# Expert results scattered to rows in token order, and read back with plain transfers in place of gathers

## The chip, the cores and the metric

The kernel runs on one core of one Trainium2 chip. The metric is the device time of one execution in microseconds (us). Five engines work side by side: TensorE (PE, with its weight loads shown as PEld), VectorE (DVE), ScalarE (ACT), GpSimd (POOL) and SyncE (SP, which only issues transfers). Transfers run on 16 DMA engines; SP's go through one queue (q1 in the profile, "hardware_dynamic"), POOL's through another (q0, "software_dynamic").

## The reference

The input is 8 sequences of 1024 rows of 256 floats (8192 tokens). Four layers follow, each with a residual sum and a layer norm:

```
x = ln(x + linear_attention(x))     # 32 heads
x = ln(x + moe0(x))                 # 8 experts, the last a no-op; top 2; capacity 1024 rows per expert
x = ln(x + attention(x))            # softmax attention, one head of 256
x = ln(x + moe1(x))                 # 8 small experts and a shared one
```

In `moe0` each of the seven real experts takes the first 1024 tokens that chose it, computes `relu(x @ w_in) @ w_out` for them, and the result, times the token's gate, is added to the token. A token's first or second choice that found no room, or that was the no-op expert, adds nothing from that expert's product. So a token has two result rows to add, of which either may be absent.

## The kernel before

All floating products are split into a high and a low part of the operands and take three fp32r matmuls each (`product`, L114 to L121; `accumulate`, L124).

**Stage A** (`stage_a`, L182 to L822, some 0 to 433 us of the span) does the first layer and the routing of the second, one sequence of 1024 rows per step, eight steps and two shorter ones for what lags behind. The order of units within a step is written out by hand (`ORDER`, L194), and every engine follows it in its own program. POOL begins with constants (L392 to L434), then subtracts to make `xT_lo` (`split_xT`, L437), adds the bias to the loaded rows (`bias`, L442) and marks slots (`mark`, L449). The router gives each chosen pair a slot number: expert times 1024 plus position, or a row of zeros past the end (`TRASH`) where there is no room. The slots are stored to memory, 8 KB a step (L359). An inverse table `inv` (128 x 56), slot to token, is built with matmuls: POOL marks in which lane and column each of the 16 x 128 pairs of the step lies (`mark_slots`, L332), ACT multiplies the column marks by the row number (L528, one instruction) and by the tile number (L530, eight instructions of 128 x 112, since the tile number is the same for a token's first and second choice), PE multiplies both together (unit "inv", L805 to L811), and DVE adds the step to `found` (`invert`, L614; the last step writes `inv`). On PE "inv" stands at the end of a step, and "slots" and the next step's "nd" follow it.

**Stage B** (`stage_b`, L825 to L1098, 433 to 789 us) runs the seven experts. POOL gathers an expert's 1024 rows by `inv`, eight indirect transfers of 128 rows (`load_rows`, L931), PE transposes them and does both products, DVE copies the results out of PSUM (`store_pairs`, L1009), and SP stores them in two halves of 512 KB in slot order (L913 to L916). During the last expert the weights of stage C are loaded and split. The first sequence's slots and gates are loaded at the start (L920, L921).

**Stage C** (`stage_c`, L1101 to L1879, 789 to 2082 us) does the rest, one sequence per step, again by a hand-written `ORDER` (L1115). For the next sequence POOL gathers the two result rows of every token by the slots, 16 indirect transfers of 128 rows (`gather`, L1342), where only two of eight tiles have a place (`GATHER = 2`), so that each pair of transfers from the third tile on waits for DVE's `combine` two tiles before it (L1538 to L1550: two scalar_tensor_tensor, L1546 and L1548, and bn_stats). POOL then does 32 subtractions for hidden activations (`split`, L1356, instruction L1361) and one bias sum (L1366). The first sequence's 16 gathers stand at the start of the stage (L1380) and land in `x2` and `x3`. SP loads wqT, wkT, the x1 rows of the first sequence (L1318 to L1320) and biases; `keep` on ACT (L1398) scales x1 rows before `combine` may start. A stage ends, and the next begins, when all engines are done with it.

Of the kernel before, what the change touches and what calls it, by code (L numbers as in the profile page):

```python
# [27 lines left out]
I32 = mybir.dt.int32  # L28
# [153 lines left out]
def stage_a(nc, d, inv):  # L182
# [63 lines left out]
    with ExitStack() as ctx:  # L246
# [19 lines left out]
        zeros = sb("zeros", [P, C])  # L266
# [32 lines left out]
        counting, first_ids = sb("counting", [P, P]), sb("first_ids", [P, 1 + TILES + P], I32)  # L299
        place_i, place = sb("place_i", [P, 2, PAIRS], I32), sb("place", [P, 2, PAIRS])  # L300
        row_at, tile_at, eights = sb("row_at", [P, 1]), sb("tile_at", [P, TILES]), sb("eights", [P, TILES])
        in_lane, in_column = sb("in_lane", [P, PAIRS, P], BF16), sb("in_column", [P, PAIRS, PLACES], BF16)
        ids = sb("ids", [P, PAIRS, 2, PLACES], BF16)
        found, partial = sb("found", [P, PLACES]), sb("partial", [P, PLACES])
# [38 lines left out]
        def _(sp):  # L343
# [41 lines left out]
            sp.wait_ge(slots_stored, 32 * BATCHES)  # L385

        @block.gpsimd
        def _(pool):
# [34 lines left out]
            const(pool.memset(eights[:], float(TILES)))  # L423
            pool.memset(in_column[:], 0.0).then_inc(marked, 1)
            const(pool.iota(first_ids[:, 1 + TILES:], pattern=[[1, P]], base=0, channel_multiplier=0))
            const(pool.iota(first_ids[:, 0:1], pattern=[[0, 1]], base=0, channel_multiplier=1))
            const(pool.iota(first_ids[:, 1:1 + TILES], pattern=[[1, TILES]], base=-TILES, channel_multiplier=0))
# [3 lines left out]
            const(pool.tensor_copy(tile_at[:], first_ids[:, 1:1 + TILES]))  # L431
            const(pool.tensor_copy(counting[:], first_ids[:, 1 + TILES:]))
# [16 lines left out]
            def mark(i):  # L449
# [5 lines left out]
                pool.tensor_tensor(tile_at[:], tile_at[:], eights[:], ALU.add).then_inc(tile_stepped, 1)  # L455
# [6 lines left out]
            pool.dma_start(d["ys"][TRASH:TRASH + P, :], zeros[:]).then_inc(zero_filled, 16)  # L462
# [9 lines left out]
            pool.wait_ge(zero_filled, 16)  # L472

        @block.scalar
        def _(act):
# [6 lines left out]
            def body(i):  # L482
# [4 lines left out]
                for unit in order(i):  # L487
# [35 lines left out]
                    elif kind == "ids":  # L523
# [5 lines left out]
                        for t in range(TILES):  # L529
                            last = act.activation(ids[:, t:PAIRS:TILES, 1, :], in_column[:, t:PAIRS:TILES, :], ACT.Copy, scale=tile_at[:, t:t + 1])  # L530
# [20 lines left out]
        def _(v):  # L551
# [5 lines left out]
            def route(i, bank, n):  # L557
# [12 lines left out]
                if not (isinstance(i, int) and i == 0):  # L570
                    v.wait_ge(slots_stored, 32 * i)
# [42 lines left out]
            def invert(i, bank, n):  # L614
# [5 lines left out]
                out = inv if isinstance(i, int) and i > BATCHES else found  # L620
                v.tensor_tensor(out[:], bank[:, 0:PLACES], partial[:], ALU.add).then_inc(inv_added, 1)
# [91 lines left out]
            body(BATCHES + 1)  # L713

# [110 lines left out]
def stage_b(nc, d, later, first_slots, first_gates, inv):  # L825
# [11 lines left out]
    with ExitStack() as ctx:  # L837
# [49 lines left out]
        def _(sp):  # L887
# [16 lines left out]
            def body(e, end):  # L904
# [15 lines left out]
            sp.dma_start(first_slots[:].rearrange("p a t -> p (a t)"), d["slots"][0:P, :]).then_inc(first_in, 16)  # L920
# [5 lines left out]
            sp.wait_ge(first_in, 32)  # L926
            sp.wait_ge(results_stored, 32 * REAL)

        @block.gpsimd
        def _(pool):  # L930
# [5 lines left out]

            load_rows(0)
# [4 lines left out]
            for e in range(1, REAL):  # L942
                pool.wait_ge(bank_full, PROLOGUE if e == 1 else group(e - 2, OUT_B))
# [985 lines left out]
```

## Time and profile before

| what | us |
|---|---|
| median of 3 runs | 2080.05 (2079.16 to 2084.12) |
| the profiled execution, whole | 2083.66 |
| its span, first to last instruction | 2081.9 |
| PE busy | 1879.4 |
| DVE busy | 1411.5 |
| ACT busy | 874.7 |
| POOL busy | 750.4 |

The mean granted TensorE clock is 0.957 of full speed. Times of rows are counted from the start of the span. A timeline row gives start, duration, engine, line, operation, output and input, count, and in brackets how long the engine had been idle and who released it. A row of waits gives the sum of the idle time, how often, and the longest.

### The profile page before, as it was taken

How to read it: one execution, taken by the hardware profiler on the slowest of the kernel's cores; microseconds unless marked ns; L12 is line 12 of the kernel's file. 1: busy time of each engine (PE TensorE's matmuls, PEld its weight loads, DVE VectorE, ACT ScalarE, POOL GpSimd, SP SyncE). 2: the span in 40 equal slices, each digit the busy share in tenths (PEclk: the TensorE clock that was granted, in tenths of full speed). 3: DMA queues.
4: the chain of work that ended last, by engine and by line, in shares of the span. 5: the costliest groups of instructions: out<-in, count | busy, mean ns of one | idle time of the engine just before them, and what ended most of it. 6: DMA issues, size and time to landing. Idle time of an engine off the chain costs nothing.

```text
span 2081.9 us, 35664 instructions
## 1 busy us (share of the span) xinstructions
PE 1879.4 (90%) x11696; PEld 1646.3 (79%) x11728; DVE 1411.5 (68%) x3599; ACT 874.7 (42%) x1623; POOL 750.4 (36%) x774
## 2 busy tenths in 40 slices
PE   7999898549999994999989989989999989989987
PEld 6888787438899993878878878878878878878876
DVE  4777777644444444687787787787787787787666
ACT  3344543423332332444534534544544544544433
POOL 4144553631111105145145145145145145144033
PEclk9999999769999996999999999999999999999999
DMA  3111112132222233012112112112112112211011
GB/s 107 62 61 61 61 61 61 42 122 82 81 81 81 81 102 115 26 52 80 34 52 80 34 52 79 34 52 78 35 53 78 35 53 78 35 53 52 11 41 62
DMA packets 80860, 129.94 MB, mean 62 GB/s; under 512 B 11184, under 2 KB 62000, under 8 KB 80720
## 3 DMA queue, kind: packets, MB, share of 16 engines
q1 hardware_dynamic: 71840, 103.91, 14.9%
q0 software_dynamic: 8880, 24.26, 5.0%
q8 instruction: 75, 1.23, 0.2%
q14 instruction: 65, 0.53, 0.1%
HBM read 103.48 MB, written 24.67 MB: 62 GB/s over the span
## 4 chain that ended last, share of the span: by engine, by line
PE 32%; DVE 15%; issue 7%; ACT 4%; POOL 2%; DVEq 0%; ACTq 0%; DMA 0%; POOLq 0%
PE c_ps L118 7%; PE c_ps L120 6%; PE c_ps L119 6%; PE c_ps L127 3%; PE c_ps L128 2%; PE c_ps L129 2%; PE c_ps L1789 2%; DVE c_shared_place L1706 2%; POOL c_place L1361 2%; DVE c_key L97 1%; DVE c_tmp L97 1%; DVE c_neg_max L1638 1%; DVE c_pre L1548 1%; DVE c_place L1619 1%; PE c_ps L1850 1%
## 5 line engine op out<-in xcount | busy, mean ns | idle before, releaser
L1361 POOL TENSOR_TENSOR c_place<-c_shared_place,c_place 128x512 fp32r<-128x512 f32 x256 | 329.1, 1310 | 376.2 <-DVE c_shared_place L1706 226.6
L1352 POOL DMA_INDIRECT c_gathered<-expert_results,c_slots x112 | 111.8, 998 | 360.5 <-DVE c_pre L1548 340.3
L1706 DVE SCALAR_TENSOR_TENSOR c_shared_place<-c_ps,c_shared_place 128x512 f32<-128x512 f32 x256 | 170.1, 683 | 31.7 <-ACT c_shared_place L1491 30.9
L127 PE MATMUL c_ps<-c_downT_hi,c_place 128*128 128x256 f32 x512 | 150.2, 293 | 16.9 <-POOL c_place L1361 16.9
L118 PE MATMUL c_ps<-c_place 128*128 128x256 f32 (+1 forms) x520 | 149.0, 287 | 17.1 <-DVE c_place L1724 10.0
L1499 ACT ACTIVATE c_place<-c_shared_place 128x512 fp32r<-128x512 f32 x128 | 80.3, 630 | 179.6 <-DVE c_shared_place L1706 178.6
L119 PE MATMUL c_ps<-c_place 128*128 128x256 f32 (+1 forms) x520 | 147.6, 284 | 0.0
L120 PE MATMUL c_ps<-c_place 128*128 128x256 f32 (+1 forms) x520 | 147.5, 284 | 0.0
L1448 ACT ACTIVATE c_shared_place<-c_ps,c_shift_s 128x1024 f32<-128x1024 f32 x64 | 71.4, 1116 | 178.5 <-DVE c_shift_s L1642 164.5
L128 PE MATMUL c_ps<-c_downT_lo,c_place 128*128 128x256 f32 x512 | 142.2, 278 | 0.0
L129 PE MATMUL c_ps<-c_downT_hi,c_place 128*128 128x256 f32 x512 | 142.2, 278 | 0.0
L933 POOL DMA_INDIRECT b_xs<-x_rows,expert_tokens x56 | 58.9, 1052 | 214.3 <-PE b_ps L1059 183.9
L118 PE MATMUL c_ps<-c_x3T_hi,c_upT_hi 128*128 128x512 f32 x256 | 106.7, 417 | 25.1 <-DVE c_shared_place L1706 25.1
L120 PE MATMUL b_ps<-b_wout_hi,b_hT_lo 128*128 128x256 f32 x448 | 126.9, 283 | 1.4 <-issue 1.4
L119 PE MATMUL b_ps<-b_wout_lo,b_hT_hi 128*128 128x256 f32 x448 | 126.8, 283 | 1.4 <-issue 1.4
L118 PE MATMUL b_ps<-b_wout_hi,b_hT_hi 128*128 128x256 f32 x448 | 127.4, 284 | 0.3
L1491 ACT ACTIVATE c_shared_place<-c_ps 128x512 f32<-128x512 f32 x128 | 75.7, 596 | 106.4 <-DVE c_shared_place L1706 54.6
L127 PEld LDWEIGHTS c_ps<-c_downT_hi,c_place 128*128 128x128 f32 x512 | 96.6, 189 | 27.0 <-POOL c_place L1361 23.9
L118 PEld LDWEIGHTS c_ps<-c_place 128*128 128x128 f32 x520 | 100.1, 192 | 21.6 <-issue 10.1
L1698 DVE SCALAR_TENSOR_TENSOR c_shared_place<-c_ps,c_x2T 128x512 f32<-128x512 f32 x128 | 86.4, 685 | 39.4 <-PE c_ps L120 28.3
L1024 DVE SCALAR_TENSOR_TENSOR b_hT_lo<-b_ps,b_hT_hi 128x512 fp32r<-128x512 f32 x112 | 75.8, 688 | 50.8 <-ACT b_hT_hi L972 49.4
L119 PE MATMUL c_ps<-c_x3T_lo,c_upT_hi 128*128 128x512 f32 x256 | 106.1, 414 | 0.0
(373 smaller groups left out, 6101.9 us busy)
## 6 DMA issues: line engine op xcount, KB each, us to landing
c_x2T<-score_rows SPq DMA_DIRECT2D x64, 512.0 KB, 5.5
a_xT_raw<-xT SPq DMA_DIRECT2D x8, 1024.0 KB, 6.6
a_x_rows<-x SPq DMA_DIRECT2D x8, 1024.0 KB, 5.6
x_rows<-a_x SPq DMA_DIRECT2D x8, 1024.0 KB, 4.4
c_pre<-x_rows SPq DMA_DIRECT2D x8, 1024.0 KB
out<-c_x SPq DMA_DIRECT2D x16, 512.0 KB
b_win_raw<-w_in SPq DMA_DIRECT2D x7, 1024.0 KB, 5.5
b_wout_raw<-w_out SPq DMA_DIRECT2D x7, 1024.0 KB
```

What stands on the lines that cost most here:

```text
L118: pe.matmul(out, lh, rh, start=(j == 0), stop=False)
L119: pe.matmul(out, lh, rl, start=False, stop=False)
L120: last = pe.matmul(out, ll, rh, start=False, stop=(j == len(terms) - 1))
L127: pe.matmul(out, lh, rh, start=False, stop=False)
L128: pe.matmul(out, lh, rl, start=False, stop=False)
L129: last = pe.matmul(out, ll, rh, start=False, stop=(stop and j == len(terms) - 1))
L1024: v.scalar_tensor_tensor(hT_lo[:, h, k, :], ps[:, bank, :], 0.0, f32(hT_hi[:, h, k, :]), ALU.max, ALU.subtract).then_inc(bank_free, 1)
L1352: pool.indirect_dma_start(rows[:, a, :], None, d["ys"], bass.IndirectOffsetOnAxis(ap=slots[:, a, t:t + 1], axis=0), bounds_check=TRASH + P ...
L1361: pool.tensor_tensor(hid_lo[:, place, :], square[:, place % RING, :], f32(hid_hi[:, place, :]), ALU.subtract).then_inc(hid_split, 1)
L1499: act.activation(hid_hi[:, place, :], square[:, place % RING, :], ACT.Copy).then_inc(hid_hi_done, 1)
L1698: v.scalar_tensor_tensor(square[:, place % RING, :], ps[:, s_bank(unit, k), :], 0.0, score_rows[:, bass.ts(e, HALF)], ALU.max, ALU.mult).t ...
L1706: v.scalar_tensor_tensor(square[:, place % RING, :], ps[:, s_bank(unit, k - lag), :], 0.0, factor, ALU.max, ALU.mult).then_inc(s_free, 1)
```

## The change

Stage A no longer stores the slots. It numbers pairs and not tokens: the inverse table now holds 1 + the row at which a result belongs, row = sequence x 2048 + tile x 256 + choice x 128 + lane. The tile number so differs for first and second choice, and ACT's eight instructions of 128 x 112 become sixteen of 128 x 56. After the last step seven DVE instructions on 128 x 56 make two tables of it: `homes`, the row of the pair (past the end where a slot is empty), and `inv`, the token. Since absent results must read as zero, POOL fills the whole result tensor (16384 rows, 16.8 MB) with zeros, 16 transfers of 1 MB, from a tile `zeros` that grows from 128 x 256 to 128 x 2048.

Stage B stores results with 56 indirect transfers of 128 rows from POOL, four per half expert, in place of SP's 14 plain ones, and POOL's last waits for their landing. The gathers of expert e + 2 stand between the two halves of expert e.

Stage C's gathers are gone. SP loads each tile's 256 rows with one plain transfer of 256 KB; the first sequence's with two of 1 MB, ahead of wqT, wkT and x1. In a step the first two tiles are loaded after the x1 rows, the other six behind the store of the sequence before.

```diff
-        zeros = sb("zeros", [P, C])
+        zeros = sb("zeros", [P, 2 * SEQ])
@@ stage_a, SP
-                sp.dma_start(d["slots"][bass.ds(i * P, P), :], slots[:].rearrange("p a t -> p (a t)")).then_inc(slots_stored, 16)
@@ stage_a, POOL
-            const(pool.iota(first_ids[:, 0:1], pattern=[[0, 1]], base=0, channel_multiplier=1))
-            const(pool.iota(first_ids[:, 1:1 + TILES], pattern=[[1, TILES]], base=-TILES, channel_multiplier=0))
+            const(pool.iota(first_ids[:, 0:1], pattern=[[0, 1]], base=1, channel_multiplier=1))
+            const(pool.iota(first_ids[:, 1:1 + PAIRS], pattern=[[1, 2], [2, TILES]], base=-PAIRS, channel_multiplier=0))
             split_xT(1)
-            pool.dma_start(d["ys"][TRASH:TRASH + P, :], zeros[:]).then_inc(zero_filled, 16)
+            ZERO_FILLS = 2 * TOKENS * C // (P * 2 * SEQ)
+            for part in range(ZERO_FILLS):
+                pool.dma_start(d["ys"].rearrange("(a p r) c -> a p (r c)", p=P, r=2 * SEQ // C)[part, :, :], zeros[:]).then_inc(zero_filled, 16)
             split_xT(2)
@@ stage_a, ACT
                         act.activation(ids[:, :, 0, :], in_column[:], ACT.Copy, scale=row_at[:, 0:1])
-                        for t in range(TILES):
-                            last = act.activation(ids[:, t:PAIRS:TILES, 1, :], in_column[:, t:PAIRS:TILES, :], ACT.Copy, scale=tile_at[:, t:t + 1])
+                        for k in range(PAIRS):
+                            last = act.activation(ids[:, k, 1, :], in_column[:, k, :], ACT.Copy, scale=tile_at[:, k:k + 1])
@@ stage_a, DVE, after body(BATCHES + 1)
+            chain = Chain(v, inv_chain, BATCHES + 1)
+            chain.step(v.tensor_scalar(empty[:], found[:], 0.0, 2.0 * TOKENS + 1.0, ALU.is_equal, ALU.mult))
+            chain.then(v.scalar_tensor_tensor, home_i[:], found[:], -1.0, empty[:], ALU.add, ALU.add)
+            chain.then(v.tensor_scalar, token_i[:], home_i[:], 8, None, ALU.arith_shift_right)
+            chain.step(v.tensor_scalar(low_i[:], home_i[:], P - 1, None, ALU.bitwise_and))
+            chain.step(v.tensor_copy(homes[:], home_i[:]))
+            chain.then(v.tensor_scalar, token_i[:], token_i[:], TOKENS // P - 1, None, ALU.bitwise_and)
+            chain.then(v.scalar_tensor_tensor, inv[:], token_i[:], float(P), low_i[:], ALU.mult, ALU.add)
+            chain.wait()
@@ stage_b, SP
-                for h, at in ((0, ROWS), (1, EACH)):
-                    sp.wait_ge(bank_free, group(e, at) if h == 0 or not end else group(e, EACH - 2 * CH))
-                    sp.dma_start(d["ys"][bass.ds(e * CAP + h * HALF, HALF), :].rearrange("(t p) c -> p t c", p=P),
-                                 results[:, bass.ts(h, HTILES), :]).then_inc(results_stored, 16)
@@ stage_b, POOL
+            def spread_results(e, h):
+                pool.wait_ge(bank_free, group(e, EACH if h and e < REAL - 1 else EACH - 2 * CH if h else ROWS))
+                for t in range(HTILES * h, HTILES * (h + 1)):
+                    pool.indirect_dma_start(d["ys"], bass.IndirectOffsetOnAxis(ap=homes[:, e * TILES + t:e * TILES + t + 1], axis=0),
+                                            results[:, t, :], None, bounds_check=2 * TOKENS - 1, oob_is_err=False).then_inc(results_stored, 16)
-            for e in range(1, REAL):
-                pool.wait_ge(bank_full, PROLOGUE if e == 1 else group(e - 2, OUT_B))
-                load_rows(e)
+            pool.wait_ge(bank_full, PROLOGUE)
+            load_rows(1)
+            for e in range(REAL):
+                spread_results(e, 0)
+                if e + 2 < REAL:
+                    pool.wait_ge(bank_full, group(e, OUT_B))
+                    load_rows(e + 2)
+                spread_results(e, 1)
+            pool.wait_ge(results_stored, 16 * TILES * REAL)
@@ stage_c, SP
+            def load_results(b, tiles):
+                for t in tiles:
+                    rows, arrived = rows_of(b, t)
+                    if t >= GATHER:
+                        sp.wait_ge(combined, TILES * b + t - GATHER + 1)
+                    sp.dma_start(rows, d["ys"][bass.ds(b * 2 * SEQ + t * 2 * P, 2 * P), :].rearrange("(a p) c -> p a c", p=P)).then_inc(arrived, 16)
             def body(b, end):
                 if not end:
                     sp.wait_ge(x2_done, HALVES * (b + 1))
-                    load_slots(b + 1)
+                    load_gates(b + 1)
                     load_rows(b + 1)
+                    load_results(b + 1, range(GATHER))
                 if not is_first(b):
                     store(b - 1, 1)
+                if not end:
+                    load_results(b + 1, range(GATHER, TILES))
                 spread_scores(b, 0)
...
+            for h in range(HALVES):
+                sp.dma_start((x2, x3)[h][:].rearrange("p (t a) c -> p t a c", a=2),
+                             d["ys"][bass.ts(h, SEQ), :].rearrange("(t a p) c -> p t a c", p=P, a=2)).then_inc(first_in[h], 16)
             sp.dma_start(wqT_raw, d["wqT1"].rearrange("(a p) n -> p a n", p=P)).then_inc(wqk_in, 16)
@@ stage_c, POOL
-            def gather(b):
...
-            gather(0)
             add_bias(0)
```

## Rows read from the trace of the kernel before

**Rows 1.** The page: busy time of the engines, share of the span, instructions.

```profile
PE 1879.4 (90%) x11696; PEld 1646.3 (79%) x11728; DVE 1411.5 (68%) x3599; ACT 874.7 (42%) x1623; POOL 750.4 (36%) x774
```

**Rows 2.** Windows: stretch, length, busy PE, PEld, DVE, ACT, POOL, clock, DMA share, GB/s.

```profile
787.00:822.00 35.00, 6.80 (x35) 6.35 (x36) 18.60 (x65) 9.76 (x22) 17.89 (x27) 0.57 0.43 132
...
1134.00:1290.00 156.00, 147.05 (x898) 127.58 (x901) 120.11 (x311) 71.68 (x135) 61.81 (x49) 0.99 0.19 55
```

**Rows 3.** Waits of the whole span: us in total, times, longest.

```profile
POOL c_gathered L1352 <- DVE c_pre L1548: 340.3, 42, 18.8
...
PE a_ps L810 <- ACT a_ids L530: 33.9, 8, 12.5
...
PE c_ps L127 <- POOL c_place L1361: 16.9, 16, 1.9
```

**Rows 4.** Source rows of L1352 and L1548 (duration min/median/max), then a timeline of stage C.

```profile
L1352 POOL DMA_INDIRECT c_gathered<-expert_results,c_slots x112: 992/998/1019, 828.2 to 1831.3; - x112
...
L1548 DVE SCALAR_TENSOR_TENSOR c_pre<-c_gathered,c_gates,c_pre x56: 483/485/1403, 848.3 to 1848.2; 128x256 f32<-128x256 f32 x56
...
1061.24 5.63 POOL L1361 TENSOR_TENSOR c_place<-c_shared_place,c_place 128x512 fp32r<-128x512 f32 x4 [9.94 <-DVE c_shared_place L1706]
...
1064.30 1.40 DVE L1548 SCALAR_TENSOR_TENSOR c_pre<-c_gathered,c_gates,c_pre 128x256 f32<-128x256 f32 x1
```

**Rows 5.** Timeline of POOL at the start of stage A.

```profile
4.23 1.80 POOL L421 MEMSET a_in_lane<- 128x2048 bf16 x1
...
8.09 5.42 POOL L440 TENSOR_TENSOR a_xT_lo<-a_xT_raw,a_xT_hi 128x512 fp32r<-128x512 f32 x4
```

**Rows 6.** Timeline of ACT: the eight tile-number instructions, and four of another width.

```profile
112.77 2.32 ACT L530 ACTIVATE a_ids<-a_in_column,a_tile_at 128x112 bf16<-128x112 bf16 x8
...
831.92 1.71 ACT L1398 ACTIVATE c_pre<-c_pre,c_gates 128x256 f32<-128x256 f32 x4 [0.90 <-DVE c_gates L1536]
```

**Rows 7.** Windows: a stretch behind PE's wait in the second step of stage A.

```profile
164.00:166.00 2.00, 1.51 (x17) 1.54 (x18) 0.00 (x0) 0.34 (x2) 0.69 (x1) 0.50 0.00 0
```

**Rows 8.** Timeline of PE and DVE at the end of stage A.

```profile
416.09 1.65 PE L810 MATMUL a_ps<-a_ids,a_in_lane 128*128 128x112 bf16 x16 [4.37 <-ACT a_ids L530]
...
430.57 1.65 PE L810 MATMUL a_ps<-a_ids,a_in_lane 128*128 128x112 bf16 x16 [12.50 <-ACT a_ids L530]
...
432.51 0.22 DVE L621 TENSOR_TENSOR expert_tokens<-a_ps,a_partial 128x56 uint32<-128x56 f32 x1
```

**Rows 9.** The page's DMA queues (packets, MB, share), then timelines around the zero fill.

```profile
q1 hardware_dynamic: 71840, 103.91, 14.9%
q0 software_dynamic: 8880, 24.26, 5.0%
...
41.64 0.73 POOL L462 DMA_DIRECT2D expert_results<-a_zeros  x1
70.37 5.02 POOL L440 TENSOR_TENSOR a_xT_lo<-a_xT_raw,a_xT_hi 128x512 fp32r<-128x512 f32 x4 [28.00 <-ACT a_xT_hi L480]
78.21 4.64 POOL L446 TENSOR_TENSOR a_x_rows<-a_x_rows,a_bias_p 128x2048 f32<-128x2048 f32 x1 [2.82 <-DMA a_x_rows<-x]
...
72.71 0.37 SPq L351 DMA_DIRECT2D a_x_rows<-x  x1
...
88.65 0.68 DVE L682 TENSOR_TENSOR a_rows<-a_ps,a_x_rows 128x512 f32<-128x512 f32 x1
```

**Rows 10.** Timelines and chain across the end of stage B and the start of C.

```profile
786.28 0.39 SPq L915 DMA_DIRECT2D expert_results<-b_results  x1
...
789.69 0.20 POOL L1334 MEMSET c_ident<- 128x128 f32 x1 [97.32 <-POOLq L837]
...
798.45 3.30 ACT L1398 ACTIVATE c_pre<-c_pre,c_gates 128x256 f32<-128x256 f32 x8 [3.92 <-DMA c_pre<-x_rows]
...
811.89 2.96 DMA c_x<-expert_results,c_slots
...
814.88 0.48 DVE L1546 SCALAR_TENSOR_TENSOR c_pre<-c_x,c_gates,c_pre 128x256 f32<-128x256 f32 x1 [0.44 <-DMA c_x<-expert_results,c_slots]
```

More of the change, by code:

```diff
@@ L179, with stage_a @@
 TOP_STEPS = 11
-def stage_a(nc, d, inv):
+def stage_a(nc, d, inv, homes):
     NDT = 2
@@ L454, in mark @@
                     pool.wait_ge(places_found, i + 1)
-                pool.tensor_tensor(tile_at[:], tile_at[:], eights[:], ALU.add).then_inc(tile_stepped, 1)
+                pool.tensor_tensor(tile_at[:], tile_at[:], sixteens[:], ALU.add).then_inc(tile_stepped, 1)
                 if not last:
@@ L471, in _ @@
                 mark(i)
-            pool.wait_ge(zero_filled, 16)
+            pool.wait_ge(zero_filled, 16 * ZERO_FILLS)
         @block.scalar
@@ L619, in invert @@
                 v.wait_ge(inv_chain, i)
-                out = inv if isinstance(i, int) and i > BATCHES else found
-                v.tensor_tensor(out[:], bank[:, 0:PLACES], partial[:], ALU.add).then_inc(inv_added, 1)
+                v.tensor_tensor(found[:], bank[:, 0:PLACES], partial[:], ALU.add).then_inc(inv_added, 1)
                 v.wait_ge(inv_added, i + 1)
@@ L822, in _, with stage_b @@
             body(BATCHES + 1)
-def stage_b(nc, d, later, first_slots, first_gates, inv):
+def stage_b(nc, d, later, first_gates, inv, homes):
     EACH = 2 * ICH + HTILES // 2 + 2 * CH + HTILES // 2
@@ L1098, in _, with stage_c @@
             body(REAL - 1, True)
-def stage_c(nc, d, weights, slots, gates):
+def stage_c(nc, d, weights, gates):
     HALVES = 2
@@ L1208, in stage_c @@
         s_full, s_free = sem("s_full"), sem("s_free")
-        slots_in, gates_in, x1_in = sem("slots_in"), sem("gates_in"), sem("x1_in")
-        first_in = [sem(f"first_in{t}") for t in range(TILES)]
+        gates_in, x1_in = sem("gates_in"), sem("x1_in")
+        first_in = [sem(f"first_in{h}") for h in range(HALVES)]
         rows_in = [sem(f"rows_in{j}") for j in range(GATHER)]
@@ L1281, in _, with load_gates @@
         def _(sp):
-            def load_slots(b):
-                sp.dma_start(slots[:].rearrange("p a t -> p (a t)"), d["slots"][bass.ds(b * P, P), :]).then_inc(slots_in, 16)
+            def load_gates(b):
                 sp.dma_start(gates[:].rearrange("p a t -> p (a t)"), d["gates"][bass.ds(b * P, P), :]).then_inc(gates_in, 16)
@@ L1340, in _ @@
                                base=0, pattern=[[-1, P]], channel_multiplier=1).then_inc(consts, 1)
-            def gather(b):
-                for t in range(TILES):
-                    rows, arrived = rows_of(b, t)
-                    producer, upto = (slots_in, 16 * b) if t < GATHER or is_first(b) else (combined, TILES * b + t - GATHER + 1)
-                    if not isinstance(upto, int):
-                        pool.to_reg(upto)
-                    pool.wait_ge(consts, CONSTS)
-                    wait_past(pool, producer, upto)
-                    for a in range(2):
-                        pool.indirect_dma_start(rows[:, a, :], None, d["ys"],
-                                                bass.IndirectOffsetOnAxis(ap=slots[:, a, t:t + 1], axis=0),
-                                                bounds_check=TRASH + P - 1, oob_is_err=False).then_inc(arrived, 16)
             def split(b, kind, j, k):
@@ L1368, in body @@
             def body(b, end):
-                if not end:
-                    gather(b + 1)
                 for h in range(HALVES):
@@ L1883, in program @@
     d["x1"] = nc.dram_tensor("x1_rows", (TOKENS, C), F32).ap()
-    d["ys"] = nc.dram_tensor("expert_results", (REAL * CAP + P, C), F32).ap()
-    d["slots"] = nc.dram_tensor("slot_rows", (BATCHES * P, 2 * TILES), U32).ap()
+    d["ys"] = nc.dram_tensor("expert_results", (2 * TOKENS, C), F32).ap()
     d["gates"] = nc.dram_tensor("gate_rows", (BATCHES * P, 3 * TILES), F32).ap()
@@ L1889, in program @@
         inv = ctx.enter_context(nc.sbuf_tensor("expert_tokens", [P, REAL * TILES], U32))
-        stage_a(nc, d, inv)
+        homes = ctx.enter_context(nc.sbuf_tensor("expert_homes", [P, REAL * TILES], U32))
+        stage_a(nc, d, inv, homes)
         shapes = {"wv": [P, CH, C + 2], "gateT": [P, CH, EXPERTS], "fc1T": [P, CH, LATENT], "fc2T": [P, 1, C],
@@ L1893, in program @@
         weights = {name: tuple(ctx.enter_context(nc.sbuf_tensor(f"c_{name}_{part}", shape, F32R)) for part in ("hi", "lo")) for name, shape in shapes.items()}
-        first_slots, first_gates = (ctx.enter_context(nc.sbuf_tensor(f"c_{name}", [P, n, TILES], dt)) for name, n, dt in (("slots", 2, U32), ("gates", 3, F32)))
+        first_gates = ctx.enter_context(nc.sbuf_tensor("c_gates", [P, 3, TILES], F32))
         stage_b(nc, d, [(d[name], hi[:, :, 0:C], lo[:, :, 0:C]) if name == "wv" else (d[name], hi, lo) for name, (hi, lo) in weights.items()],
-                first_slots, first_gates, inv)
-        stage_c(nc, d, weights, first_slots, first_gates)
+                first_gates, inv, homes)
+        stage_c(nc, d, weights, first_gates)
 def kernel(**inputs):
```

29 lines of the change are left out of this document (14 added, 15 removed).

## The prediction

> **What bounds the kernel now.** I began with the busy shares: PE works 90% of the span, POOL 36% [rows 1]. So work taken from POOL pays only where PE waits for POOL. The windows say where the 10% are: a step of stage C keeps PE busy 147 of 156 us at a granted clock of 0.99, while the change from stage B to C leaves it 6.8 of 35 us at 0.57 [rows 2]. Then the waits. The largest sum beside the gathers is POOL's own: 340 us in which it waits for DVE's combine, because only two tiles fit [rows 3]. The gathers are early, then, and DVE is the late one. In the steps of C no row of waits has DVE or PE waiting for a gathered tile. One gather keeps POOL 0.998 us and hardly varies over 112; when the first hidden subtraction of a step starts, at 1061.24, POOL had been idle 9.94 us, waiting for DVE [rows 4]. So 14 us of POOL per step lie wholly in its own idle time.
>
> **What the change takes away.** The 112 gathers of the steps of C, 112 us of POOL: worth 0, covered by the 340 us of waiting [rows 3, 4]. The store and loads of the slots, 8 KB each on SP: 0, nobody waits for them. In B, 14 stores leave SP: 0 except at the end (below).
>
> **What it adds, in order of time.**
>
> Constants: `zeros` grows to 2048 columns of 4 bytes. The nearest row is 2048 columns of 2 bytes, 1.80 us; the old 256 columns cost about an eighth, 0.3. POOL runs without a gap from there to its first subtraction at 8.09 [rows 5], on which the first matmul hangs. I take +1.5 us, the width in columns deciding; if bytes decide, +3.3.
>
> ACT's tile numbers: eight instructions of 112 columns take 2.32 us, 0.29 each; four of 256 columns with a scale operand take 1.71, 0.43 each [rows 6]. That is 0.96 ns per column, so 56 columns come to 0.236 and sixteen to 3.8 us: +1.5 us per batch. Bounds: 0, if cost went with columns alone; +2.3, if 56 cost what 112 do. Nothing hides it: PE waits for just this instruction in 8 of 9 steps, 33.9 us in all [rows 3], and behind "inv" on PE stand "slots" and the next step's "nd". 8 x 1.5 = 12.0 us. In the step where it doesn't wait I count nothing. The long wait has the clock at 0.50 behind it already [rows 7]; I add nothing for that.
>
> End of A: the last two batches are among the eight, PE waits there 4.37 and 12.5 us, and DVE's table ends the stage at 432.7 [rows 8]. Seven more DVE instructions of 128 x 56, at 0.22 each and a little between, all ahead of the gathers of B: +1.7 us.
>
> Zero fill: 16.8 MB. The hardware queue moved 103.9 MB in 14.9% of 2081.9 us, 335 GB/s [rows 9]; by that it takes 50 us, from 42 to about 92. POOL's sixteen issues, at 0.73 [rows 9] to 1.0 [rows 4] and a gap, take 12 to 21 us of the 28.0 us in which POOL is idle, so they cost 0 unless the queue fills. But the x rows of the second sequence are asked for at 72.71, in the midst of it. They now land by 78.21; POOL's bias takes 4.64, DVE wants it at 88.65 [rows 9], so landing may slip by 5.8 us. If they landed only with the last zeros, at 92, DVE would be 8 us late; behind it stand the rest of the step's evictions, and PE, which can be up to eight banks ahead of it, would feel only a part. Bounds 0 and 8 us; I take 2, nearer to 0 because of that lead.
>
> The Trainium skill ("DMA: Bandwidth & Descriptors", Queues, rings and completion order) says that each DMA engine takes turns between queues by whole packets. The trace shows mean packets of 2.7 KB on POOL's queue and 1.45 KB on SP's [rows 9], and no heavy traffic on both at once. By this rule the x rows, in 1 KB packets, get between a fifth and a ninth of the bandwidth and come with the last zeros; the sum would be up to 6 us higher. That is a rival below.
>
> Stage B: 56 scatters of about 1.0 + 0.3 us are 73 us of POOL beside its 73 us of gathers, in the 357 us from 432.7 to 789.69 [rows 8, 10]. A half expert's four take 5.2 us, an expert 51 us; DVE needs the place back only when the next expert's same half is done. Cost 0. The gathers of e + 2 move behind four scatters, 5.2 us later, but have most of an expert to land: 0. The same skill ("SBUF — State Buffer", Two separate sides) warns that POOL cannot write descriptors while DVE holds the port they share. Over 112 indirect transfers beside a busy DVE the trace has 992 to 1019 ns [rows 4], so it does not show here; by the page some scatters would take longer, still inside the 51 us.
>
> End of B, uncovered: now SP issues the last half at 786.28 and stage C starts at 789.69, 3.4 us. Sixteen gathers between 789.69 and the last start at 811.89 give at most 1.39 us each, and the last lands after 2.96 [rows 10]. Four scatters: 3 x 1.39 + 2.96 + 0.2 = 7.3, so +3.9 us. Bounds +1 (a faster landing) and +7.
>
> Start of C: the 16 gathers look like the gain, but DVE loses only 0.44 us to the last of them [rows 10]; it works through its two halves meanwhile. What starts it is `keep` at 798.45, 8.8 us into the stage, when the x1 rows have landed [rows 10]. Now 2.1 MB go ahead of them on the same queue: 6.3 us at 335 GB/s. Before, five gathers (0.65 MB, 2 us) had shared that time. 6.3 - 2.0 - 0.4 = +3.9 us; bounds 0 and +6.
>
> The steps of C: six of eight tiles are loaded behind SP's store of the sequence before, and that store is ready when combine 0 has run; a load of 256 KB then has the time that two gathers had. 0.
>
> **Sum.** 1.5 + 12.0 + 1.7 + 2.0 + 3.9 + 3.9 = 25.0 us. The profiled execution took 2083.7 us (span 2081.9), which would become 2108.7; it lies 3.6 above the median, so for the median I predict 2080.05 + 25.0 = 2105. It can be told from no change beyond 0.3%, 6.2 us.
>
> **Rivals.**
>
> *The zero fill starves or blocks stage A.* For it: half of one 50 us transfer backlog stands ahead of a load with 5.8 us to spare, and POOL, if its queue takes no more before zeros have drained, comes late to the subtraction at 70.37, which PE needs at once. Against: ACT, not POOL, opens that one now. Price 8 to 20 us more than the 2 taken: 2111 to 2123. Chance 0.15.
>
> *Small instructions are cheap and the ends short.* Sixteen halves cost the eight wholes (-12), or scatters and loads land fast (-6). 2087 to 2097. Chance 0.13.
>
> *POOL's relief pays.* In each step DVE's two-operand instructions stretch from 0.485 to 1.40 us while POOL is busy [rows 4], and PE waits for POOL's subtraction, 16.9 us in all [rows 3]. If gathers were the cause of both, 8 steps would give back 16.9 + 8 x 1.5 = 29 us, and the kernel would end at 2105 - 29 = 2076; it decides from 3.1 us per step. Against: the stretched one lies inside POOL's subtractions [rows 4], which stay, and no gather runs there. Chance 0.09: 0.04 for faster by over 6 us, 0.05 within.
>
> *The gathers' waits only change hands.* SP is now one queue for rows, scores and stores; if combine waited 2 to 3 us per step for a load stuck behind a store, 7 steps add 18: 2123. No row shows SP late. Chance 0.03.
>
> The forecast itself, 2098 to 2112, has 0.60. From it and the rivals: slower 0.91, same 0.05, faster 0.04. The range 2090 to 2123 leaves out the gain and the far ends.
>
> **What would show it.** Right: the sixteen ACT instructions at 3.8 us a batch and PE waiting 1.5 us longer at L810 in each; POOL's first subtraction at 9.6; stage C starting 7 us behind the last eviction and `keep` 12 to 13 us into it; steps of C still 156 us apart. Wrong: steps of C shorter than 155, DVE waiting for x rows between 85 and 100 us by more than 6, POOL stuck in its fills past 70, or sixteen halves at 2.4 us.

## The result, and the profile after

The changed kernel takes 2132.15 us (median of 4, 2131.02 to 2136.34) against 2079.61 (2078.76 to 2084.12): 1.0249 times as long, 95% interval 1.0231 to 1.0267. The prediction was +25 us with a range up to 2123; it is +52.5, and 2132 lies beyond the range. The direction was right, the size half. The page of after, where it answers to [rows 1, 9]:

```profile
PE 1908.4 (90%) x11728; PEld 1676.5 (79%) x11728; DVE 1415.2 (66%) x3606; ACT 888.9 (42%) x1695; POOL 698.1 (33%) x717
...
q1 hardware_dynamic: 79456, 113.22, 15.9%
q0 software_dynamic: 7680, 31.47, 3.9%
```

PE is still 90% busy of a longer span (2130.3 us) and 29 us busier, with the same products. Most of that is a slower clock: 0.937 of full speed was granted, 0.957 before. To see where the time lies I cut the span at SP's first issue of a stage. For the kernel before I use a second profile of it, run e5_before_again below (span 2076.2), because the first one (2081.9) had a stage B 5.8 us longer than that of the second, with the same kernel: nothing that the change does.

| stretch | before | after | difference | predicted |
|---|---|---|---|---|
| stage A | 433.5 | 466.6 | +33.1 | +17.2 |
| stage B | 350.7 | 362.4 | +11.7 | +3.9 |
| start of C, to the next sequence's loads | 31.4 | 35.0 | +3.6 | +3.9 |
| rest of C | 1260.6 | 1266.3 | +5.7 | 0 |
| sum | 2076.2 | 2130.3 | +54.1 | +25.0 |

Stage A scatters from one execution to the next. In the seven traces of this record whose stage A is that of the kernel before it takes 433.1 to 442.2 us, so the 433.5 above is near the low end, and a few of the 33.1 us can be scatter. A second trace with the stage A of the changed kernel (e4) has 465.7.

Three things stand out in the trace. First, PE's waits in stage A, answering to [rows 3]:

```profile
PE a_ps L821 <- ACT a_ids L532: 46.1, 8, 14.0
PE a_ps L118 <- POOL a_xT_lo L440: 11.9, 1, 11.9
```

PE's wait for POOL's first subtraction, the second line, was 9.5 us before. The wait for the tile numbers grew by 12.2 us, as the step said. But the middle steps are 51.3 us apart instead of 47.9, so 3.4 us each and not 1.5. The windows show the rest. Before, in one step of the first profile: up to the wait's end, the stretch at a granted clock of 0.50, and what follows (columns as in [rows 2]):

```profile
256.00:262.60 6.60, 3.41 (x45) 3.17 (x44) 3.74 (x9) 5.10 (x13) 4.97 (x4) 1.00 0.00 0
262.60:269.40 6.80, 6.80 (x29) 6.41 (x29) 5.52 (x29) 0.00 (x0) 0.00 (x0) 0.50 0.19 35
269.40:276.00 6.60, 6.60 (x39) 5.68 (x39) 5.46 (x18) 5.24 (x11) 3.52 (x1) 1.00 0.77 284
```

And after, in the same step:

```profile
276.00:280.60 4.60, 2.18 (x19) 1.98 (x17) 3.51 (x7) 4.60 (x13) 4.01 (x4) 1.00 0.00 0
280.60:294.30 13.70, 11.45 (x60) 10.52 (x61) 8.04 (x40) 2.70 (x11) 1.25 (x2) 0.50 0.33 111
294.30:301.00 6.70, 6.70 (x41) 5.80 (x40) 4.75 (x11) 6.13 (x13) 6.70 (x8) 1.00 0.22 89
```

A wait of 3.19 us had 6.8 us at 0.50 (1.2 GHz) behind it; one of 4.67 us has 13.7, of which 2.3 are still idle. PE works 11.4 us there at half speed instead of 6.8, which is 2.3 us of work lost. With the 1.5 us of longer wait that makes 3.8 us, where 3.4 are measured.

Second, the x rows of the second sequence (timelines of SP, POOL and DVE, answering to [rows 9]):

```profile
79.15 0.37 SPq L352 DMA_DIRECT2D a_x_rows<-x  x1
...
44.88 8.60 POOL L464 DMA_DIRECT2D expert_results<-a_zeros  x16
76.80 5.02 POOL L440 TENSOR_TENSOR a_xT_lo<-a_xT_raw,a_xT_hi 128x512 fp32r<-128x512 f32 x4 [23.32 <-ACT a_xT_hi L482]
94.56 4.62 POOL L446 TENSOR_TENSOR a_x_rows<-a_x_rows,a_bias_p 128x2048 f32<-128x2048 f32 x1 [12.74 <-DMA a_x_rows<-x]
...
99.31 0.69 DVE L683 TENSOR_TENSOR a_rows<-a_ps,a_x_rows 128x512 f32<-128x512 f32 x1 [4.15 <-POOL a_x_rows L446]
```

The rows take 15.4 us from issue to POOL's bias, 5.5 before; DVE waits 4.15 us. POOL's sixteen issues are cheap, 8.60 us in its idle time, so POOL is not what was blocked. The last zeros land at 92.3. Until then the two queues alternate; here are the packets and MB of each from 84 to 90 us:

```profile
q0 software_dynamic: 302, 2.21, 88.7%
q1 hardware_dynamic: 301, 0.31, 14.5%
```

For each packet of zeros, most of them of 8 KB, one of 1 KB of the x rows goes through. So the x rows get an eighth of the bytes and come through only when the zeros end.

Third, the end of stage B. The source rows of the line that opens the stage's block (duration in ns, min/median/max, then first and last start):

```profile
L848 POOLq COMPARE_BRANCH  x1: 41/41/41, 819.4 to 819.4; - x1
L848 POOLq DRAIN  x1: 9200/9200/9200, 819.5 to 819.5; - x1
```

And the timelines of DVE and POOL around it, answering to [rows 10]:

```profile
811.60 0.69 DVE L1032 COPY b_results<-b_ps 128x512 f32<-128x512 f32 x1 [5.00 <-PE b_ps L120]
...
816.94 0.98 POOL L945 DMA_INDIRECT expert_results<-b_results,expert_homes  x1 [0.30 <-issue]
828.98 0.20 POOL L1364 MEMSET c_ident<- 128x128 f32 x1 [11.06 <-POOLq L848]
```

The last scatter has landed at 819.4, and for 9.2 us every engine waits for a DRAIN instruction on POOL with which a block ends. It is counted as busy in no view; it shows only among the rows of the line on which the block is opened.

### The profile page after: what moved, and what is told of

Read it like the earlier page. It is cut to its first block, busy times and chain, and to the rows that moved or that the text cites. A ratio compares the mean times of both kernels' runs of the same rounds, so it can differ in the third digit from the quotient of the medians.

```text
span 2130.3 us, 35652 instructions
## 1 busy us (share of the span) xinstructions
PE 1908.4 (90%) x11728; PEld 1676.5 (79%) x11728; DVE 1415.2 (66%) x3606; ACT 888.9 (42%) x1695; POOL 698.1 (33%) x717
## 4 chain that ended last, share of the span: by engine, by line
PE 31%; DVE 16%; issue 7%; ACT 4%; POOL 2%; DVEq 0%; DMA 0%; ACTq 0%; SPq 0%; POOLq 0%
PE c_ps L118 6%; PE c_ps L120 6%; PE c_ps L119 6%; PE c_ps L127 3%; PE c_ps L129 2%; PE c_ps L128 2%; PE c_ps L1802 2%; DVE c_shared_place L1719 2%; POOL c_place L1377 2%; DVE c_neg_max L1651 1%; DVE c_tmp L97 1%; DVE c_key L97 1%; DVE c_pre L1561 1%; DVE c_place L1632 1%; DVE c_pre L1559 1%
## 5 line engine op out<-in xcount | busy, mean ns | idle before, releaser
L1719 DVE SCALAR_TENSOR_TENSOR c_shared_place<-c_ps,c_shared_place 128x512 f32<-128x512 f32 x256 | 170.2, 683 | 32.9 <-ACT c_shared_place L1504 32.6
L945 POOL DMA_INDIRECT expert_results<-b_results,expert_homes x56 | 57.0, 1018 | 202.7 <-DVE b_results L1032 188.3
L120 PE MATMUL c_ps<-c_x3T_hi,c_upT_lo 128*128 128x512 f32 x256 | 107.1, 419 | 0.0
```

The costliest lines, as they stand in the source:

```text
L120: last = pe.matmul(out, ll, rh, start=False, stop=(j == len(terms) - 1))
L1719: v.scalar_tensor_tensor(square[:, place % RING, :], ps[:, s_bank(unit, k - lag), :], 0.0, factor, ALU.max, ALU.mult).then_inc(s_free, 1)
```

## Experiments

Each run stands beside the kernel before on its own chip. Stage times are read from the profiles as above. Two runs, as e1 to e4 have, tell little by themselves: the intervals of e3 (1.0172 to 1.0258) and e4 (1.0176 to 1.0269) overlap that of the changed kernel, and what these two show is read from their traces.

**e1_before_ids16: the kernel before with sixteen instructions.**

```diff
-for t in range(TILES):
-    last = act.activation(ids[:, t:PAIRS:TILES, 1, :], ..., scale=tile_at[:, t:t + 1])
+for k in range(PAIRS):
+    last = act.activation(ids[:, k, 1, :], in_column[:, k, :], ACT.Copy, scale=tile_at[:, k % TILES:k % TILES + 1])
```

> The kernel before, with one thing of the change alone: ACT writes the tile numbers in sixteen instructions of 56 columns, not eight of 112; the values are the old ones. Theory 'low clock': each batch's instruction group takes 3.80 us, not 2.32, and the stretch at granted clock 0.50 that follows PE's wait for it grows from about 7 us to about 13.5 us, which costs some 1.9 us of PE work more in each middle step; the x rows of stage A's steps are asked for 51.3 us apart, not 47.9, and the kernel takes 20 to 25 us more than before, 2100 to 2105. Rival 'flat price' (my prediction's step): 8 x 1.5 = 12 us, steps 49.4 us apart, 2092; the rest of stage A's loss then belongs to the zero fill.

Its two runs took 2096.5 and 2110.3, before 2078.3: 1.0112, with the wide interval 1.0025 to 1.0200. In the profiled one stage A takes 452.1 us, 18.6 more. Of these 3.5 stand ahead of any tile number: the second x rows are asked for at 76.45, not 72.92. SP asks for later x rows at:

```profile
225.14 0.41 SPq L351 DMA_DIRECT2D a_x_rows<-x  x1
276.19 0.41 SPq L351 DMA_DIRECT2D a_x_rows<-x  x1
```

51.05 us apart; the stretches at 0.50 in these steps last 13.7 us. One step takes 47.4 us; the stretch at its start lasts only 3.4. No fill runs here. So the instructions alone make the long step.

**e2_after_ids8: the changed kernel with eight.** The second choice's 128 rows go into the row number.

```diff
-act.activation(ids[:, :, 0, :], in_column[:], ACT.Copy, scale=row_at[:, 0:1])
-for k in range(PAIRS): ...
+for a in range(2):
+    act.activation(ids[:, a * TILES:(a + 1) * TILES, 0, :], ..., scale=row_at[:, a:a + 1])
+for t in range(TILES): ...
```

> The changed kernel, with the tile numbers in eight instructions again and the second slot's 128 rows put into the row number instead (two instructions of 448 columns in place of one of 896), so that the result is the same. Theory 'low clock': steps of stage A return to 48 us, and the kernel takes 20 to 24 us less than the changed one, 2108 to 2112. Rival 'flat price': 11 to 12 us less, 2120. Rival 'zero fill': steps stay 51 us apart since it is something else that lowers the clock, less than 6 us gained.

2117.1, stage A 451.6: 15.0 less. Steps are 48.1 us apart and their stretches at 0.50 are 6.8 us again. Less than I expected, more than the flat price. Counted from the third request for x rows on, where the fill is over, and without the chain of seven, stage A with sixteen instructions (after, e1, e3, e4) is 13 to 19 us longer than in the kernel before; e2, with eight, is 3. So the term is 13 to 19 us, where I had 12.

**e3_after_fill_spread.**

```diff
-for part in range(ZERO_FILLS):
-    pool.dma_start(...)
 split_xT(2)
 bias(1)
+fill(0)
 with pool.Fori(1, BATCHES - 2) as i:
     split_xT(i + 2)
     bias(i + 1)
+    for k in range(3):
+        fill(i * 3 + (k - 2))
     mark(i - 1)
```

> The changed kernel, with the sixteen zero fills issued one before the loop of stage A and three in each of its five passes, behind POOL's bias, instead of all at once before the second sequence. Theory 'the fill delays the x rows': DVE's wait of 4.15 us at 95 to 99 us goes, and with it the low-clock stretch of 10 us at 106.8 that follows; step 2 begins 5 to 9 us earlier and the kernel takes 2123 to 2128. Rival 'the fill is harmless': within 2 us of 2132. Rival 'the fill hurts wherever it is': 3 MB in each step delays xT or the stores, steps of A longer than 51.3 us, 2135 or more.

2124.7 (2123.2, 2126.2); stage A 457.7, 8.9 less. DVE no longer waits for the bias, and the 10.2 us at 0.50 from 106.5 on are gone. Not all of the 8.9 is the fill's, though: only 3.1 of it are there when the third sequence's x rows are asked for (131.3 against 134.4), and 4.0 come from one step of 47.4 us, which e1 has without any fill. More traces help. The three with all fills at once (after, e2, e4) have DVE waiting 4.2 to 7.4 us for the bias and a stretch of 10.2 to 17.1 us at 0.50 begin between 102 and 107, which no other trace has. They ask for the third x rows at 134.4 to 136.5 us, the seven with the old stage A at 121.0 to 130.1. The means differ by 10.9 us, of which 2.5 are the constants: 8.4 for the fill, and 2 to 13 by single traces. Three fills in each of five passes cost nothing that can be seen: the steps between take 47.4 to 51.1 us, with the numbers' price in them.

**e4_after_no_drain.** Stage B's block is opened without POOL's drain; all its transfers are awaited by semaphores first.

```diff
-block = ctx.enter_context(nc.Block())
+block = ctx.enter_context(nc.Block(no_gpsimd_drain=True))
```

> The changed kernel, whose stage B ends without the DRAIN instruction on POOL (all its scatters and gathers have been awaited by their semaphores before). Theory 'the drain': the 9.2 us DRAIN on POOL that stands between the last scatter's landing and stage C goes, C starts some 9 us earlier and the kernel takes 2122 to 2124. Rival 'the scatters' landing': the 16.7 us between the last eviction and stage C are the time the last rows take to be written and acknowledged; then the wait on the results' semaphore takes it over and the time stays at 2132. Rival 'moved': stage C pays the 9 us at its first POOL instruction or gather instead, 2132.

Stage B takes 352.9 us, 9.5 less, and nothing takes the place of the drain there. The runs took 2124.2 and 2128.5, 2 us more than the theory allowed in the median: 3.0 of the 9.5 were given back in the first step of C (157.0 us, 154.0 after the drain); why is open. What is left between the last eviction and stage C:

```profile
810.46 0.69 DVE L1032 COPY b_results<-b_ps 128x512 f32<-128x512 f32 x1 [5.00 <-PE b_ps L120]
...
818.62 0.20 POOL L1364 MEMSET c_ident<- 128x128 f32 x1 [1.83 <-POOLq L848]
```

818.62 - 811.15 = 7.5 us. My step had 7.3 for the four scatters.

**e6_before_late_pool: what the drain waits for.**

```diff
     load_rows(e)
+pool.wait_ge(bank_free, group(REAL - 1, EACH - 2 * CH))
+pool.memset(ident[:, 0:1], 0.0).then_inc(ident_done, 1)
+pool.wait_ge(ident_done, 3)
```

> The kernel before, with one memset of a column put at the end of POOL's part of stage B, behind the last eviction: the gathers, 100 us earlier, stay where they are. Theory 'the drain has a price of its own': the DRAIN on POOL takes 9 to 11 us again, now after the last eviction, and stage C starts 7 to 9 us later, 2086 to 2089. Rival 'the drain waits for what is under way': with nothing under way it takes under 1 us and the time stays at 2079.

```profile
L837 POOLq DRAIN  x1: 4632/4632/4632, 786.7 to 786.7; - x1
```

Neither theory: 4.6 us, 93 us after the last gather. Stage C starts 5.2 us behind the last eviction, not 3.4, and the kernel takes 2082.8 against 2079.4 (1.0010, interval 0.9998 to 1.0023). In the kernel before the same DRAIN takes 11.2 us, right behind the gathers and a hundred us ahead of the stage's end, where it costs nothing; in stage A, without indirect transfers, it takes 0.3 us there and 1.5 us after the fills. That could mean that it depends on how fresh the indirect transfers are. The DRAIN at the end of the kernel speaks against it, in the kernel before and in e4:

```profile
L1152 POOLq DRAIN  x1: 10784/10784/10784, 2064.8 to 2064.8; - x1
...
L1169 POOLq DRAIN  x1: 10772/10772/10772, 2105.3 to 2105.3; - x1
```

The last indirect transfer lies 233 us back in the first and 1289 us in the second, which had no DRAIN at the end of stage B. In the changed kernel, which had one, the DRAIN at the end takes 1.6 us. So it is long where indirect transfers were issued since the last DRAIN, however long ago; e6 with its 4.6 us fits neither this nor freshness. What POOL does in it is open.

**e5_before_again: the kernel before, unchanged.**

> The kernel before, unchanged, for a second profile of it: its runs so far lie at 2078 and at 2084 us, and the profile shown lies at the upper of the two. Theory 'a state of stage B': in an execution near 2078 the middle steps of stage B are 46.5 us apart instead of 47.7, and nothing else differs; the 7 us that the changed kernel's stage B seems to gain on the profile of before are then no effect of the change. Rival: B's steps are 47.7 us in it as well, and the scatters do take something away from B's steps.

Ratio 0.9999. The w_in loads of stage B (SP) show it:

```profile
550.93 0.39 SPq L889 DMA_DIRECT2D b_win_raw<-w_in  x1
597.45 0.39 SPq L889 DMA_DIRECT2D b_win_raw<-w_in  x1
```

46.5 us a step, 47.7 in the profile that I predicted from, where PE paused once in each step in the middle of a product, for 0.4 to 0.7 us and for no wait. Whoever compares that profile with the one of after sees a gain of 7 us in stage B that isn't one.

**e5_c_alone, e13_c_alone_again: stages A and B of before, stage C as changed.** The results still stand in slot order, so stage C adds wrong rows; the transfers are those of the change.

```diff
-sp.dma_start(rows, d["ys"][bass.ds(b * 2 * SEQ + t * 2 * P, 2 * P), :]...)
+sp.dma_start(rows, d["ys"][bass.ds(b * HALF + t * 2 * P, 2 * P), :]...)
```

> Stages A and B of the kernel before, with stage C as changed: its result rows come by plain transfers. It leaves out the right rows: each sequence reads 2048 rows from row 512 b on. Theory 'stage C of its own': the first loads of C are followed by those of the next sequence after 35 us instead of 32, and the steps of C are 157.0 us apart instead of 156.2, some 8 to 9 us in all, 2087. Rival 'phase': the steps are 156.2 us and the 157.0 of the changed kernel come from when C begins; then 2082. Rival 'relief': POOL freed of its gathers, the steps get shorter, under 2078.

> The kernel with stage C alone changed once more (wrong rows as before), now on the same chip as the others of this call. Theory 'places': steps of C 156.7 to 157.1 us again, 2088 to 2092. Rival 'chip or execution': 156.2, 2085.

1.0059 (1.0041 to 1.0077) and 1.0058 (1.0037 to 1.0079), that is 12 us. The start of C takes 35.7 us in both, against 31.4: +4.3. The steps behind the first are 156.6 to 157.4 us, and all that follows the start of C takes 6.2 us more. These two profiles also have 4 and 3 us more in stage A, which is unchanged: scatter. Waits hardly explain them: PE waits 1.6 us longer for POOL in all eight steps together, and for nothing else. Matching the two traces product by product, nearly all of the delay builds up in the products with `c_downT`. One line of these, by groups with their mean ns, in e5_before_again:

```profile
L128 PE MATMUL c_ps<-c_downT_lo,c_place 128*128 128x256 f32 x512 | 142.3, 278 | 0.0
```

And the same group in e5_c_alone, 282 ns instead of 278:

```profile
L128 PE MATMUL c_ps<-c_downT_lo,c_place 128*128 128x256 f32 x512 | 144.4, 282 | 0.0
```

The change drops the table of slots, 64 bytes a partition, from between the weights that stay and the tiles of stage C. That gave the next runs.

**e8_c_alone_pad: 64 bytes put back; e12_before_pad64: 64 bytes added to the kernel before.**

```diff
+pad = ctx.enter_context(nc.sbuf_tensor("pad", [P, 2, TILES], U32))
```

> The kernel of the run with stage C alone changed, with 64 bytes a partition put where the table of slots had been, so that every tile of stage C stands at its old address. It reads the same wrong rows. Theory 'addresses': in that run PE lost its 0.7 us a step in the products with c_downT alone, a few ns in each, with nothing waited for; with the tiles back at their places the steps are 156.2 us apart again, 5 us less than without the 64 bytes, some 2086. Rival 'traffic': the plain transfers or the missing gathers do it, the steps stay at 156.9, 2091.

> The kernel before, with 64 unused bytes a partition between the persistent weights of stage C and its tiles; no instruction, transfer or wait is another. Theory 'distance': what costs PE a few ns in each product with c_downT is how far the tiles stand from the weights; the steps of C go from 156.2 to 156.9 us and the kernel takes 5 us more, 2084. Rival 'only nearer costs': 64 bytes further apart are harmless, 156.2 and 2079. Rival 'traffic': what slowed stage C was never the places; 156.2 and 2079 as well, and then the run with stage C alone must repeat its 156.9 only by chance.

With the gap restored the steps are 156.1 us and the products 278 ns; 2088.3 against 2087.0 on that chip, 1.0005 (0.9989 to 1.0021). With 64 unused bytes added to the kernel before, not one instruction being another:

```profile
1293.60 0.46 SPq L1285 DMA_DIRECT2D c_gates<-gate_rows  x1
1450.50 0.47 SPq L1285 DMA_DIRECT2D c_gates<-gate_rows  x1
```

156.9 us a step, products of 283 ns, and 2086.7 against 2079.8: 1.0031 (1.0016 to 1.0046). This settles it: the steps of C are longer because of where tiles lie, not because of gathers or loads. Why the place matters to a product is open.

**e7_before_dve_ids, e15_before_dve_ids_again: the numbers off ACT.** Since PE waits for them in every step, I tried them elsewhere in the kernel before.

```diff
-act.activation(ids[:, :, 0, :], in_column[:], ...)
-for t in range(TILES): ... .then_inc(ids_done, 1)
+act.activation(ids[:, :, 0, :], in_column[:], ...).then_inc(ids_done, 1)
...
+elif kind == "ids":
+    v.tensor_tensor(ids[:, :, 1, :]..., in_column[:]..., tile_at[:].unsqueeze(1).unsqueeze(3).to_broadcast(...), ALU.mult).then_inc(tiles_done, 1)
```

> The kernel before, with the tile numbers written by DVE in one instruction of 896 columns, ahead of its eviction of the third projection, while ACT writes the row numbers; the result is the same. Theory 'PE's wait and the low clock behind it': the wait of 33.9 us in 8 steps shrinks by 8 x 2.3 us, the stretches at 0.50 behind it shrink or go, steps of stage A come 3 to 5 us closer; 18 to 35 us less, 2045 to 2061. Rival 'only the wait': 8 x 2.3 = 18 us less, 2061. Rival 'DVE is late': its eviction behind the new instruction holds PE, less than 10 us gained.

> The kernel before with DVE's tile numbers once more, for its interval: its runs so far lie at 2061 and 2069. Expected 8 to 16 us below the kernel before, 0.992 to 0.996 of it, and below or level with the mended kernel: it has neither the scatters at the end of stage B nor the chain of seven.

0.9934 (0.9910 to 0.9958) and 0.9932 (0.9908 to 0.9955): 2068.9 and 2066.4. That is 10 to 13 us, less than the 18 that the shorter wait alone should give. The instruction takes 2.2 us in five of the nine batches, and PE now waits for what stands behind it on DVE (waits of stage A, e7):

```profile
PE a_ps L814 <- DVE a_ids L706: 16.9, 2, 10.3
PE a_ps L765 <- DVE a_mix L666: 16.2, 6, 6.8
```

Steps are 46.1 us, and 44.5 to 45.1 in some of e15.

**e9_after_mended, e10_mended_again, e11_mended_pad96, e14_mended_pad64: the changed kernel with its side costs removed.** e3's spread with the wide memset behind the second bias, e4's block, e7's numbers, and stage C's first loads in another order.

```diff
+first_results(0)
 ... wqT, wkT
 load_rows(0)
+first_results(1)
```

> The changed kernel with its four mended places: the tile numbers by one instruction of 896 columns on DVE; the fills spread over stage A and the wide memset put behind the second bias; no DRAIN on POOL at the end of stage B; stage C's loads in the order first half of the results, wq, wk, x1, second half. Result the same. By the runs so far: 2132 - 27 (tile numbers) - 9 (fills) - 9.5 (drain) - 2 (memset) - 3 (order) = 2082, range 2074 to 2092; stage A 430 to 436 us, stage C's first loads to the next sequence's 32 us instead of 35. Theory 'the change itself has nothing to give': even mended it stays above the kernel before with DVE's tile numbers (2069), by the scatters at the end of B and the chain of seven. Rival 'it pays once mended': under 2065.

> The mended kernel of the run before once more, for its stage B: there, with nothing changed in PE's instructions of that stage, its middle steps took 54.7 us, not 46.6, PE pausing in the middle of products for no wait while POOL's gathers ran. Theory 'a state of the execution or the chip, as the 47.7 us of the kernel before is': steps are 46.6 us here, and the kernel takes some 50 us less, 2068 to 2075. Rival 'the kernel's own': 54.7 us again and 2118, so that something among the four mendings starves PE in stage B.

> The mended kernel with 96 bytes a partition added ahead of stage C's tiles. In the changed kernel they stand 160 bytes above their old places, with it 256. Theory 'addresses', with places that matter by less than 256 bytes: steps of C 156.1 us instead of 157.0, 6 us less than the mended kernel of the same call. Rival 'other places or other cause': 157.0 and no difference.

> The mended kernel with 64 bytes a partition ahead of stage C's tiles: the weights stand 224 bytes above their old places, and now the tiles do too, where the 96 bytes put them 256 above. Theory 'distance': the steps of C are 156.1 to 156.3 us, and the kernel takes 5 to 6 us less than the mended one, 2068 to 2076, below the kernel before. Rival 'absolute places': 157.0 and no difference, 2078.

e9 came to 2118.6, on a chip on which before took 2087.0, far off my 2082. The start of C (32.1) was as expected, and stage A (426.4) shorter than the 430 to 436. Stage B took 393.5 us, though PE's instructions there are those of before. PE's waits in its loop:

```profile
PE b_ps L119 <- issue: 8.8, 14, 1.5
PE b_ps L120 <- issue: 8.7, 13, 1.1
```

And PE's timeline while gathers run:

```profile
602.55 0.28 PE L119 MATMUL b_ps<-b_wout_lo,b_hT_hi 128*128 128x256 f32 x1 [0.68 <-issue]
...
605.42 0.28 PE L119 MATMUL b_ps<-b_wout_lo,b_hT_hi 128*128 128x256 f32 x1 [0.92 <-issue]
```

PE stops inside products, with nothing waited for, and the low clock follows. The same kernel on another chip (e10) has none of it: steps of 46.6 us, stage B 353.0, 2078.6, ratio 0.9996 (0.9982 to 1.0009). It is the 47.7 us of the first profile in a worse form, and its cause stays open: it was not tried which chip, or which place of the program in memory, brings it. The chip is a plausible rival: e8, on the same chip as e9, has steps of 47.7 us with the same short pauses as the first profile (whose chip is not known), and no other trace has any. e11's 96 bytes were miscounted: the change moves the weights too, by the 224 bytes of the new table, so the gap became 32 bytes wider than in the kernel before, not equal to it; steps of 156.9, no gain. e14's 64 bytes restore the gap: 156.2 us a step, and 2075.6, ratio 0.9965 (0.9947 to 0.9983).

So the change, mended, can be had for less than the kernel before; but what wins there is DVE's numbers. The kernel before with these alone is 9 us faster still, 2066.4 on the same chip (e15), though the intervals of the two ratios overlap a little. The profiles differ by 14.7 us (2074.4 and 2059.7): stage A 9.8 (426.5 and 416.7, of which much is scatter: e10 and e11, with e14's stage A, have 418.5 and 422.3), stage B 2.1 (353.0 and 350.9), stage C 2.8, at its start and in its first step. Nothing in C comes back.

## Why the prediction was wrong, step by step

- **The steps of C get nothing from POOL's relief:** right. Gathers were worth 0. But "The steps of C ... 0" missed 5.7 us: the removed table moves tiles by 64 bytes relative to the weights (e12: 64 bytes alone cost 1.0031).
- **ACT's numbers, 12.0:** the durations were exact, 3.80 us a batch (sixteen: 0.24 us each) and 12.2 us more waiting. The step that failed is "the long wait has the clock at 0.50 behind it already; I add nothing for that". The stretch doubled, to 13.7 us in the middle steps, and the term is 13 to 19.
- **Zero fill, 2.0, bounds 0 and 8:** 8.4 as a mean over traces, 8.9 by e3, with several us of scatter. The step that failed is "nearer to 0 because of that lead": the landing slipped by 9.9 us, DVE waited 4.15, and PE's lead did not keep it from the extra stretch at 0.50. The rival that had it right in kind, *the zero fill starves stage A*, got 0.15. The x rows came with the last zeros: 15.4 us from issue to bias, at 94.56, while the last fill was issued at 53 and took 39.9 us to land. That is what the Trainium skill ("DMA: Bandwidth & Descriptors", Queues, rings and completion order) states with its turns of whole packets, and the trace agrees: 302 packets against 301.
- **Constants, 1.5:** the memset was 1.80 as taken, by columns. POOL's first subtraction came 2.45 us later: 1.5 from the memset, and 0.9 in one small select that took 1.12 us where it had taken 0.20. All four traces with the wide memset ahead of it have this (1.12 to 1.21 us), and none of the others; its cause is open.
- **End of A, 1.7:** 1.4: the table is there at 464.72, the last of the seven ends at 466.10.
- **End of B, +3.9:** the scatters were right, 7.5 us instead of 3.4. The step left out what the block does when POOL is last: 9.5 us of DRAIN (e4). Its row, 11.2 us, was in the trace before, hidden.
- **Start of C, +3.9:** right, +3.6; `keep` starts 12.7 us into the stage, 12 to 13 was forecast. Splitting the loads gives 2.4 to 2.9 back (e9, e14: 32.1 and 32.6).
- **The sum.** 2.5 + 17 + 8.9 + 1.4 in stage A is 29.8 of 33.1, with 17 and 8.9 each uncertain by several us. The other 3 lie within the scatter of stage A: the 6.8 us at 0.50 from 41.6 on, say, are in neither profile of the kernel before, but e5_c_alone, e6 and e12, whose stage A is the same, have such stretches. Then 9.5 + 4.1 - 1.9 in B, 3.6 and 5.7 in C: 54. The 1.9 I can't name.

*Small instructions are cheap*: fell with e1 and e2. *POOL's relief pays* and *the gathers' waits only change hands*: fell with e5_c_alone.

## What to carry over

A wait on the engine that bounds the kernel is not priced by its length: look at the stretch of low clock behind the nearest such wait, and count that it may double. If an engine becomes the last one to finish a stage, look up what it does at the stage's end; its closing DRAIN is counted nowhere as busy and may have been hidden. When a change adds or removes a buffer, compare with a version that keeps every other buffer's place. And take several traces of the same code before a few microseconds of a stage are read as an effect: stage A alone scatters by 9.

## What the runs showed that I had not expected

- POOL's DRAIN at a block's end: 11.2 us right behind gathers, 9.2 behind scatters, 10.8 at the kernel's end 233 and 1289 us after the last of them, 4.6 in e6, 0.3 to 1.6 in stages without indirect transfers.
- 64 bytes a partition more or less between weights and tiles: 278 or 282 to 283 ns for a product of 256 columns, 0.7 us in a step of 156, without a wait.
- PE pausing inside products in stage B: steps of 46.6, 47.7 or 54.7 us in kernels whose instructions on PE are the same there.
- A wait of PE of 3.2 us was followed by 6.8 us at the lower clock, one of 4.7 us by 13.7.
